# A two-layer decoder on one core: the state space stage with its convolution on TensorE, one group of look-ahead, and moved steps in the attention stages

## The reference, cut to what matters

```
xn = layernorm(x)                       (the kernel's residual form)
x_ssm, x_gate = split(xn @ in_proj_w.T + in_proj_b)
x_conv = silu(conv1d(x_ssm, 4 taps, causal, per feature) + conv_b)
B, C = split(x_conv @ bc_w.T + bc_b)    16 states
dt = softplus(x_conv @ dt_w.T + dt_b)
h_t = h_(t-1) * exp(dt_t * A) + dt_t * B_t * x_t
y_t = sum over the states of h_t * C_t, + x_t * D
out = (y * silu(x_gate)) @ out_w.T + out_b
z = out + xn;  layernorm(z) * ln_g + ln_b, added to x
```

## Time and profile before

| | |
|---|---|
| median of 3 runs | 3501.4 us (3501.36 to 3505.9) |
| profiled execution, its own time | 3496.35 us |
| its span, first to last instruction | 3494.6 us |
| PE, DVE, ACT, POOL busy | 2775.8, 2045.5, 1474.4, 1455.7 us |
| mean granted TensorE clock | 0.91 of full |
| state space stage | up to 809.4 us |
| first scores of attention b, c, e | at 842.5, 1184.7 and 2505.7 us |

### The profile page before, as it was taken

The page is one execution under the profiler, slowest core; times in us unless marked ns, Lnnn a source line. Parts: engine busy times, 40 slices in busy tenths (PEclk is TensorE's granted clock), DMA queues, the critical chain, the costliest instruction groups (busy, mean ns, idle before and its releaser), DMA issues. The chain is left out here.

```text
span 3494.6 us, 50412 instructions
## 1 busy us (share of the span) xinstructions
PE 2775.8 (79%) x16708; PEld 1904.8 (55%) x16708; DVE 2045.5 (59%) x3504; ACT 1474.4 (42%) x2585; POOL 1455.7 (42%) x1508
## 2 busy tenths in 40 slices
PE   3777777765777588868899999699588888865998
PEld 1323223223555355534788885399355555544887
DVE  3888888884887478863122224501488888882111
ACT  3555555443666365531122221222366666641222
POOL 2666666662444466626000006200145555552444
PEclk8878887987999799989999999899799999987999
DMA  9500000000003000002566663000100000004775
GB/s 331 179 1 1 0 1 0 0 0 28 13 12 124 13 1 0 1 20 105 166 195 192 193 190 93 20 1 1 33 13 26 26 26 28 29 28 136 211 210 154
DMA packets 135986, 244.90 MB, mean 70 GB/s; under 512 B 16145, under 2 KB 107793, under 8 KB 125329
## 3 DMA queue, kind: packets, MB, share of 16 engines
q1 hardware_dynamic: 115344, 208.33, 18.5%
q0 software_dynamic: 20448, 34.11, 4.0%
HBM read 154.17 MB, written 90.05 MB: 70 GB/s over the span
## 5 line engine op out<-in xcount | busy, mean ns | idle before, releaser
L506 POOL TENSOR_TENSOR u_in<-dtx,b_rep 128x512 f32<-128x512 f32 x256 | 332.2, 1318 | 233.3 <-ACT b_rep L487 224.0
L479 PE MATMUL PS<-scaled,ident 128*128 128x512 f32 x512 | 319.6, 710 | 69.5 <-DVE scaled L516 69.2
L522 DVE TENSOR_TENSOR_SCAN state<-PS,u_in 128x512 f32<-128x512 f32 x256 | 311.3, 1219 | 79.1 <-POOL u_in L506 36.7
L2085 PE MATMUL PS<-d_unit_T,d_w 128*128 128x256 f32 x1248 | 283.7, 381 | 1.0 <-ACT d_unit_T L2095 1.0
L495 ACT ACTIVATE PS<-dt,decay_rate 128x508 f32<-128x508 f32 x256 | 174.2, 685 | 247.2 <-DVE state L522 246.8
L2106 ACT ACTIVATE d_act_b<-PS 128x256 f32<-128x256 f32 (+1 forms) x188 | 78.9, 420 | 472.5 <-PE PS L2085 472.5
L1340 POOL TENSOR_TENSOR e_hs<-e_pr 128x512 f32<-128x512 f32 x128 | 162.9, 1273 | 270.0 <-ACT e_pr L1307 269.2
L2118 DVE TENSOR_TENSOR d_hid<-d_act_b,PS 128x256 f32<-128x256 f32 (+1 forms) x188 | 87.6, 467 | 316.0 <-ACT d_act_b L2106 316.0
L2085 PEld LDWEIGHTS PS<-d_unit_T,d_w 128*128 128x128 f32 x1248 | 235.1, 191 | 32.0 <-issue 1.4
L1243 DVE TENSOR_REDUCE e_mx<-PS 128x8 f32<-128x1024 f32 x128 | 156.0, 1219 | 78.7 <-PE PS L1186 78.7
L2043 PE MATMUL PS<-d_w,d_hid 128*128 128x256 f32 x880 | 199.4, 381 | 2.1 <-DVE d_hid L2118 2.1
(11 more groups left out here) (422 smaller groups left out, 6449.2 us busy)
## 6 DMA issues: line engine op xcount, KB each, us to landing
d_w<-in_d_w SPq DMA_DIRECT2D x41, 1024.0 KB, 4.9
f_w<-in_f_w SPq DMA_DIRECT2D x39, 1024.0 KB, 5.1
rows_in_place<-blank SPq DMA_DIRECT2D x136, 272.0 KB, 5.3
d_w<-in_d_w SPq DMA_DIRECT2D x41, 512.0 KB, 3.9
f_unit_rows<-rows_in_place SPq DMA_DIRECT2D x39, 272.0 KB, 5.2
rows_by_expert<-zeros SPq DMA_DIRECT2D x39, 256.0 KB, 2.8
d_unit_rows<-rows_by_expert SPq DMA_DIRECT2D x39, 256.0 KB, 3.9
out_by_expert<-d_y_rows SPq DMA_DIRECT2D x39, 256.0 KB, 4.0
```

The source lines that it names most:

```text
L479: nc.tensor.matmul(YB[:, c], ident[:], scaled[:, (KD * n + c) % RC], start=False, stop=n == NS - 1).then_inc(m_y, 1)
L506: nc.gpsimd.tensor_tensor(u_in[:, k % RU], dtx[:, p, c], b_rep[:, n % RB], ALU.mult).then_inc(m_u, 1)
L522: nc.vector.tensor_tensor_scan(state[:, k % 2], DECAY[:, k % RD], u_in[:, k % RU], 0.0, ALU.mult, ALU.add).then_inc(m_h, 1)
L2085: step = nc.tensor.matmul(b, wt[:, r, c, f * 128:f * 128 + 128], x, start=c == 0, stop=c == KD - 1)
```

## The change

In the state space stage:

- The convolution goes from DVE to TensorE: eight diagonal matrices `conv_w` (identity times a tap) are made once, and eight products accumulate in PSUM. ACT copies the result to `half_conv` and takes the tanh from PSUM, in two halves.
- The residual and the output bias are added in PSUM by two more identity products for each sequence. `xnb` and its POOL sum go away, and the copy to `z_row` goes from DVE (a sum) to ACT (a copy). `xn` has three buffers.
- `dt_u` (add one) goes from DVE to ACT. The addition to `X` goes from DVE to POOL.
- Turn g holds back(g-1), early(g+1) and late(g+1). early(1) no longer stands ahead of turn 0. All turns are written out; the hardware loop is gone.
- Nearly every `yield` has another number.
- The loads come in another order (x of group 0, then the small vectors, then the weights), with counters of their own, and the constants are made after the statistics of group 0.

In stages b, c and e only the numbers in `PLAN` and `ROUTE` change.

```diff
     def mamba_late_vector(dve, g, p):
-        link = Chain(dve, m_vec3, 7, g)
-        for c in range(KD):
-            yield 2 + 2 * c
...
-            link(nc.vector.tensor_scalar(half_conv[:, c], xpad[:, c, :, 0:L], hcw[:, 4 * c:4 * c + 1],
-                                         hcb[:, c:c + 1], ALU.mult, ALU.add))
-            for j in range(1, 4):
-                step = nc.vector.scalar_tensor_tensor(
-                    out=half_conv[:, c], in0=xpad[:, c, :, j:j + L], scalar=hcw[:, 4 * c + j:4 * c + j + 1],
-                    in1=half_conv[:, c], op0=ALU.mult, op1=ALU.add)
...
-        yield 8
...
+        yield 11
+        dve.wait_ge(m_fev2, EV2 * g + KD)
         nc.vector.scalar_tensor_tensor(out=flat(xconv[:, p]), in0=conv_tanh[:], scalar=1.0,
...
-        yield 21
-        after(dve, m_e, g + 1)
-        nc.vector.tensor_scalar(dt_u[:], dt_e[:], 1.0, None, ALU.add).then_inc(m_u1, 1)
-        yield 18
+        yield 22
         dve.wait_ge(m_u1, g + 1)
...
-        yield 24
+        yield 28
...
     def mamba_late_pool(pool, g, p):
-        yield 10
...
-        nc.gpsimd.tensor_tensor(xnb[:, p], xn[:, p], m_rows[:, 0:1].broadcast_to([128, GS, D]),
-                                ALU.add).then_inc(m_xnb, 1)
...
     def mamba_late_scalar(act, g, p):
-        yield 9
-        after(act, m_conv, KD * g + KD)
-        nc.scalar.activation(conv_tanh[:], half_conv.rearrange("p c s t -> p (c s t)"), ACT.Tanh).then_inc(m_th, 1)
-        yield 13
+        for c in range(KD):
+            yield 10 + c
+            after(act, m_conv, KD * g + c + 1)
+            after(act, m_xc, g)
+            nc.scalar.activation(half_conv[:, c], seqs(FB[:, c]), ACT.Identity, bias=hcb[:, c:c + 1])
+            nc.scalar.activation(conv_tanh[:, c * GT:c * GT + GT], FB[:, c], ACT.Tanh, bias=hcb[:, c:c + 1]).then_inc(m_fev2, 1)
+        yield 17
...
+        nc.scalar.activation(dt_u[:], dt_e[:], ACT.Copy, bias=1.0).then_inc(m_u1, 1)
...
         for m in range(2):
-            yield 18
+            yield 26
...
-        yield 25
+        yield 19
         after(act, m_u1, g + 1)
         nc.scalar.activation(dt_l[:], dt_u[:], ACT.Ln).then_inc(m_ln, 1)
 
     def mamba_late_tensor(pe, g, p):
         yield 7
+        after(pe, m_z, g)
+        after(pe, m_fev1, EV1 * g + EV1)
+        for c in range(KD):
+            for j in range(4):
+                step = nc.tensor.matmul(FB[:, c], conv_w[:, c, j], xpad[:, c, :, j:j + L], start=j == 0, stop=j == 3)
+            step.then_inc(m_conv, 1)
+        yield 10
...
     def mamba_back_vector(dve, g, p):
-        yield 1
+        yield 0
...
-        yield 6
-        after(dve, m_op, g + 1)
-        after(dve, m_zn, g)
-        nc.vector.tensor_tensor(flat(z_row), flat(FB), flat(xnb[:, p]), ALU.add).then_inc(m_z, 1)
+        yield 8
...
-        yield 16
-        after(dve, m_zb, g + 1)
-        nc.vector.tensor_tensor(X[:, g], X[:, g], z_norm[:], ALU.add).then_inc(m_x, 1)
 
     def mamba_back_tensor(pe, g, p):
-        yield 1
+        yield 0
...
+            nc.tensor.matmul(flat(FB)[:, s * D:s * D + D], ident[:], xn[:, g % 3, s], start=False, stop=False)
+            step = nc.tensor.matmul(flat(FB)[:, s * D:s * D + D], ident[:], m_rows[:, 0], start=False, stop=True)
...
     def mamba_back_scalar(act, g, p):
-        yield 12
+        yield 5
+        after(act, m_op, g + 1)
+        after(act, m_zn, g)
+        nc.scalar.activation(flat(z_row), flat(FB), ACT.Copy).then_inc(m_z, 1)
+        yield 10
...
     def mamba_back_pool(pool, g, p):
-        yield 11
+        yield 8
...
+        nc.gpsimd.tensor_tensor(X[:, g], X[:, g], z_norm[:], ALU.add).then_inc(m_x, 1)
...
             if g + 1 < NG:
+                sides.append(early(eng, g + 1, 1 - p))
                 sides.append(late(eng, g + 1, 1 - p))
-            if not isinstance(g, int) or g + 2 < NG:
-                sides.append(early(eng, g + 2, p))
...
         alone(early(eng, 0, 0))
+        if first:
+            first(eng)
         alone(late(eng, 0, 0))
-        alone(early(eng, 1, 1))
...
+        for g in range(NG):
+            turn(g, g % 2)
         alone(back(eng, NG - 1, 1))
...
-        "e": dict(front=[10, 12, 15, 18, 22, 38, 40, 55, 58, 62, 68, 72], taken=[12, 14, 8, 18, 24, 36, 38, 54, 58, 64, 66, 78],
-                  back=[2, 8], out_at=[4, 6], early=[36, 40, 44]),
+        "e": dict(front=[2, 12, 18, 18, 22, 42, 48, 52, 55, 60, 62, 70], taken=[2, 14, 6, 18, 22, 42, 46, 52, 54, 58, 64, 74],
+                  back=[0, 8], out_at=[2, 8], early=[16, 30, 48]),
```

More of the change, by code:

```diff
@@ L184, in decoder_kernel @@
     RD, RU, RC, RB = 2, 4, 4, 4
-    xn = mamba_mem.take("xn", [128, 2, GS, D])
-    xnb = mamba_mem.take("xnb", [128, 2, GS, D])
+    xn = mamba_mem.take("xn", [128, 3, GS, D])
+    conv_w = mamba_mem.take("conv_w", [128, KD, 4, 128])
     xnT = mamba_mem.take("xnT", [128, 2, KD, GT])
@@ L427, in mamba_late_tensor @@
         yield 7
+        after(pe, m_z, g)
+        after(pe, m_fev1, EV1 * g + EV1)
+        for c in range(KD):
+            for j in range(4):
+                step = nc.tensor.matmul(FB[:, c], conv_w[:, c, j], xpad[:, c, :, j:j + L], start=j == 0, stop=j == 3)
+            step.then_inc(m_conv, 1)
+        yield 10
         after(pe, m_xc, g + 1)
-        after(pe, m_z, g)
-        after(pe, m_fev1, EV1 * g + 3)
         for c in range(KD):
@@ L574, in mamba_back_pool, with mamba @@
     def mamba_back_pool(pool, g, p):
-        yield 11
+        yield 8
         link = Chain(pool, m_pool2, 4, g)
         rstd_of(pool, g, 1, link, m_mv2, m_nb2)
-        yield 13
+        yield 16
         after(pool, m_zn, g + 1)
         link(nc.gpsimd.tensor_tensor(z_norm[:], z_norm[:], m_rows[:, 1:2].broadcast_to([128, GS, D]), ALU.mult))
-        yield 11
+        yield 23
         nc.gpsimd.tensor_tensor(z_norm[:], z_norm[:], m_rows[:, 2:3].broadcast_to([128, GS, D]),
                                 ALU.add).then_inc(m_zb, 1)
+        yield 28
+        pool.wait_ge(m_zb, g + 1)
+        nc.gpsimd.tensor_tensor(X[:, g], X[:, g], z_norm[:], ALU.add).then_inc(m_x, 1)
         link.turn_over()
-    def mamba(eng, early, late, scan, back):
+    def mamba(eng, early, late, scan, back, first=None):
         def turn(g, p):
             sides = []
-            if not isinstance(g, int) or g > 0:
+            if g > 0:
                 sides.append(back(eng, g - 1, 1 - p))
-            if not isinstance(g, int) or g + 1 < NG:
+            if g + 1 < NG:
+                sides.append(early(eng, g + 1, 1 - p))
                 sides.append(late(eng, g + 1, 1 - p))
-            if not isinstance(g, int) or g + 2 < NG:
-                sides.append(early(eng, g + 2, p))
             weave(scan(eng, g, p), merged(*sides))
         alone(early(eng, 0, 0))
+        if first:
+            first(eng)
         alone(late(eng, 0, 0))
-        alone(early(eng, 1, 1))
-        turn(0, 0)
-        turn(1, 1)
-        with eng.Fori(0, (NG - 4) // 2) as pair:
-            turn(2 * pair + 2, 0)
-            turn(2 * pair + 3, 1)
-        turn(NG - 2, 0)
-        turn(NG - 1, 1)
+        for g in range(NG):
+            turn(g, g % 2)
         alone(back(eng, NG - 1, 1))
@@ L2425, in _ @@
         sp.dma_start(ident[:], ins["ident"]).then_inc(setup, 16)
-        for t, name in ((m_w_sb, "m_w"), (m_v_sb, "m_v"), (b_bc, "m_bbc"), (m_rows, "m_rows"), (selector, "m_sel")):
+        for g in range(1):
+            sp.dma_start(X[:, g], ins["x"][g * GS:g * GS + GS].rearrange("s t d -> t s d")).then_inc(x_first[g], 16)
+        for t, name in ((m_v_sb, "m_v"), (b_bc, "m_bbc")):
+            sp.dma_start(t[:], ins[name]).then_inc(m_small, 16)
+        for t, name in ((m_w_sb, "m_w"), (m_rows, "m_rows"), (selector, "m_sel")):
             sp.dma_start(t[:], ins[name]).then_inc(m_loaded, 16)
-        for g in range(NG):
+        for g in range(1, NG):
             sp.dma_start(X[:, g], ins["x"][g * GS:g * GS + GS].rearrange("s t d -> t s d")).then_inc(x_first[g] if g < 2 else x_rest, 16)
```

140 lines of the change are left out of this document (68 added, 72 removed).

## The result

| | before | after |
|---|---|---|
| median of the runs | 3501.38 us (3501.35 to 3505.9) | 3395.35 us (3395.03 to 3397.44) |
| span of the profiled execution | 3494.6 us | 3393.2 us |
| mean granted TensorE clock | 0.91 | 0.93 |
| state space stage | 843.7 us | 816.9 us |
| attention b | 315.8 | 300.2 |

What follows compares the result with a forecast made beforehand. VectorE (DVE) was taken as the bound of the state space turns. Work -76.3 and +1.9, waits +51, ahead of turn 0 -21, behind turn 7 +4.5, attention 0: -40 us, forecast 3460 us, range 3402 to 3492.

Steps and rivals of the forecast that it cites:

- the one on attention: Attention stages: blocks keep their lengths and only waits move; taken as 0, between -33 and +20 us.
- ahead of turn 0: State space stage before its first turn: first scan at 55 us instead of 76.3, -21 us, or 14 at worst.
- behind turn 7: After the last turn: output product 3.6 us longer, addition 2.3 in place of 1.2, together +4.5 us, uncovered.
- The work on VectorE: State space turns: pieces leaving VectorE take off 76.3 us, one more set of statistics adds 1.9.
- VectorE's time without work: State space turns: waits of the new order sum to 131 us against 80 before, so 51 us come back.
- The steady turn: Turns 1 to 5 of the state space stage: near 90 us each, with VectorE busy near 70.
- Those on TensorE: VectorE's waits in a turn: 5.6 us at its start behind the output block, 3.5 at the input product.
- The one on ACT: Gate copies and logarithm together behind unit 26 delay the decay of unit 27; VectorE stands 3.7 us.
- the wait at unit 9: VectorE stands 3.1 us, at worst 6.6, for POOL's end-part scale; the convolution's own 3.5 us lies under it.
- rival 1: State space waits stay 10 us a turn because pieces overlap more: 3410 us, chance 0.27.
- 2, TensorE becomes the bound at the lower level: Added TensorE records run at 1.2 GHz, VectorE waits some 10 us more a turn: +70, 3530 us; chance 0.10.
- 3, the attention order: A third of the waits for scores in stages b and e goes: 3428 us, chance 0.13.

Runs made afterwards that it cites:

- e1: The kernel before with the new PLAN and ROUTE (attention positions) alone, old state space stage: 3425.47 us, ratio 0.9784.
- e3: The kernel before with the copies of the inverted sums in the attentions written as a maximum over an axis of one element: 3459.73 us, ratio 0.9879.
- e8: The kernel after with the dt piece on VectorE behind unit 24 in place of 22: 3376.25 us, ratio 0.9637.
- e15: The kernel after with dt piece behind unit 24, logarithm behind 28, its use behind 29, GpSimd's scale behind 10, ScalarE's norm behind 13: 3351.99 us.
- e13: The kernel after with every convolution computed twice on TensorE, the second overwriting the first: 3448.07 us, ratio 0.9839.
- e2: The kernel after with the old PLAN and ROUTE (attention positions): 3473.78 us, ratio 0.9916.

## Why the prediction was right and wrong

**The step that failed** is the one on attention: "The blocks keep their lengths and change places by a few steps. This moves waits; nothing in the rows says which way. I take 0, between -33 [...] and +20." Measured -79.6 (e1 alone: 77 in the span). Two things were wrong in it. It lets an order move waits only and takes each engine's own work as fixed: VectorE's copies lasted 51 us less in sum, because the order decides whether they meet an instruction on GpSimd. Replacing them in the kernel before (e3) gives 44 us, and where these are reduces the order is worth 31 us and not 80; that part is shown. And the bound was built from one wait only, the one for scores. In e that wait gave 21.7 us, more than the third that I allowed; in b it gave 0.3. In c, which I left out, it gave 3.3, and waits for `c_oT` (10.4 to 2.1) and `c_den` (9.4 to 4.2) shrank while one for `c_x` grew (9.3 to 15.3). In e something also came back: the wait for `e_den` grew from 5.7 to 17.0, and a sum with two inputs in SBUF is held more than before:

```profile
L1276 DVE TENSOR_TENSOR e_oT<-e_part 128x128 f32<-128x128 f32 x64 | 24.6, 384 | 2.2
```

and after:

```profile
L1274 DVE TENSOR_TENSOR e_oT<-e_part 128x128 f32<-128x128 f32 x64 | 32.9, 514 | 2.2
```

That these shares add up to the stages' gains is read from the groups and waits and not tested by removing each. The row that should have warned me was in reach: the copy's group had a mean of 481 ns where single ones took 0.23.

**State space: -27 us, forecast -40.** By parts, measured against the forecast's own terms:

| | forecast | measured |
|---|---|---|
| ahead of turn 0 | -21 | -20.2 |
| turn 0 | -5 | -3.8 |
| turns 1 to 5 | 5 x -2.7 | 5 x -3.1 |
| turn 6 | -0.8 | +6.5 |
| turn 7 | -3.9 | +1.5 |
| behind turn 7 | +4.5 | +4.5 |

A forecast turn is -10.9 us of work plus the new waits less the old 10; turn 0 is -8.0 and +3, turn 7 -2.9 and 9 - 10, turn 6 has the added statistics of 1.9. The one unit of 1.9 us that went from the window of turn 0 to that of turn 7 is in the measured column: at equal units turn 0 gains 1.9 us and turn 7 0.4. So the miss is in turns 0, 6 and 7.

Two terms of the sum were mis-sized, and most of one hides the other. The work on VectorE was to fall by 76.3 - 1.9 = 74 us. From the first scan to the last gating product its busy time fell from 608.2 to 567.7 us, by 40.5. All the pieces named are gone, but what stayed became longer: the dt piece 35.8 us for 14.2, `dt_l` 16.0 for 11.2, the gate 11.1 for 8.5. (A few us more are no miss of the change: operations in a row overlap by some 0.08 us, which group sums count twice.) VectorE's time without work was to grow by 51 us, and grew from 106.6 to 135.9, by 29. So 34 us of work came back unforeseen and 22 us of waiting did not come.

The forecast also spread the old waits evenly, 10 us a turn, where the steady turns had 63.5 / 5 = 12.7 and turns 6 and 7 6.5 each. That shifts gains between the rows of the table and leaves their sum as it is. The gap between 94.2 and 84.6 was in front of me.

**The steady turn was right by two errors.** It was to lose 2.7 us and lost 3.1. But its work fell by 5.5 us (78.9 to 73.4) and not by 10.9, and its waits grew by 2.2 (12.7 to 14.9) and not by 8.2. Those on TensorE came smaller (3.80 for 5.6 and 1.10 for 3.5), where its clock was up: the skip products took 1.98 us at the upper level where I had used 3.51, and the input product 3.70. The one on ACT was 3.02 for 3.7. Against that `dt_e` took 5.77 us and not 2.17, 3.6 us a turn. The forecast had weighed contention, but priced only the addition to `X`, 3 us for all turns, and let the dt operations stand as they were. The Trainium skill, GPSIMD Engine Reference, Specifications, names contention where a VectorE instruction has two SBUF inputs; the rows agree, at a price that e8 shows to be larger.

**What was right.** The first scan (55, measured 56.15), the convolution (7.5, measured 7.0), the wait at unit 9 (3.1, measured 3.24), and that the convolution lies under that wait: e15 takes the other cause of the wait away and 3.0 of the 3.23 us stay, and e13 shows that there is no room for a second one. Ahead of turn 0 the start of 15.5 and the pieces behind it add up to 31.6 us and not the 31.8 written there, and no sum is given for the lower end of the range, 3402, which is said to be rival 1 with its 3410.

**The rivals.** 1, waits do not grow: no, they grew from 12.7 to 14.9 a turn, by less than I had. Its time of 3410 us is the nearest to the measured one, by luck, as it has nothing from the attentions. 2, TensorE becomes the bound at the lower level: no, the granted clock of turns 1 to 5 rose from 0.83 to 0.90 with more work on it. By the Trainium skill, TensorE: Matmul & The Clock Gate, Part 1, activity releases the clock; that agrees. 3, the attention order: yes in kind, stage e changed by over 10 us, but it was to be waits alone, and the size was 2.4 times the 33 us of the rival.

**What stays open.** Why `front` and `ROUTE` need each other in e is read from the wait for `e_rT` only. The some 24 us of the order that do not go through copies, and the hold's share in e beyond them (the other two-input sums on VectorE), were not tested apart. The clock was not either: e2 has the state space code of the kernel after, and in its turns 2 to 4 the skip products take 2.4 to 3.6 us and not 1.98, and no run shows why.

## What to carry to other kernels

Before costing a reorder at nothing, compare the mean of each VectorE group with its shortest instruction: where the mean is well above, look for what runs on GpSimd at that time, and try a form that doesn't need the shared ports, or a place in a pause of GpSimd. Look at what stays as well as at what is moved away: here 29 us of the work taken off VectorE came back in three operations that stayed. Take waits from the turn or stage that is changed, not from an average over unlike ones. In a woven schedule, test position tables as a set: one part alone cost 72 us in a stage where the whole gave 33. To learn how much of a gain goes through one cause, remove that cause from both kernels and compare again.

## What the runs showed of the hardware that was not expected

- A VectorE instruction with two inputs in SBUF that meets GpSimd can be held for more than the one instruction that it met: `dt_e` took 5.76 to 5.78 us instead of 1.22 in six turns, with three of GpSimd's in a row. `gate` and `dt_l` of the same form were held for one only (1.57 and 2.28 us), and then GpSimd waited for them. The Trainium skill, SBUF — State Buffer, SBUF: two separate sides, has the loser blocked for the whole of the other's instruction. `gate` and `dt_l` agree; that three can go by is what the rows of `dt_e` add, and no run shows when.
- A pair of copies of 128x128 takes 0.36 us alone and 1.45 beside one GpSimd instruction, and a copy of 128x4 elements has a mean of 1.12 us before and 0.17 after. A held copy of either size ends with the GpSimd instruction that it met, so the small one loses as much.
- A reduce over an axis of one element does the same copy in 0.27 to 0.29 us and was never held.
- TensorE's clock at one place changed with the order of the work around it: the skip products at the start of a turn took 3.4 to 3.7 us before in six of seven turns and 1.98 in all seven after, while the granted clock of turns 1 to 5 rose from 0.83 to 0.90.
